# A fused attention and expert kernel: in the last batch slot, slot reads before first-layer weights, one gather behind two scatters, table operations one step later

## The reference

```python
def reference(x, ctx, mask, g_xattn, g_ffn, adj, Wq, bq, Wk, bk, Wv, bv, Wo, bo, gate_w, w1, b1, w2, b2):
    # attention: 16 heads of 16, scores + adj, masked, softmax over 512 keys
    x = x + tanh(g_xattn[0]) * attention(layernorm(x), ctx, ctx, adj, mask, Wq, bq, Wk, bk, Wv, bv, Wo, bo)
    # experts: each token goes to the one expert with the highest gate probability
    h = layernorm(x)
    probs = softmax(h @ gate_w.T)                  # [2048, 8]
    e, p = argmax(probs), max(probs)
    y = (relu(h @ w1[e] + b1[e]) @ w2[e] + b2[e]) * p
    return x + tanh(g_ffn[0]) * y
```

## Time and profile before

| | |
|---|---|
| median of 3 runs | 548.91 us (548.83 to 552.67) |
| profiled execution, its own time | 550.53 us |
| its span in the profile | 548.5 us |
| granted clock of PE over the span | 0.998 |
| PE busy | 526.3 us, 96% |
| VectorE, ACT, POOL busy | 302.3, 309.1, 297.9 us |
| the last slot's attention ends | about 369.6 us |
| late tiles | from 414 us to the end |

### The profile page before, as it was taken

One profiled execution on the slowest core, in us unless ns is written; L12 is line 12 of the kernel. 1 busy time (PEld: TensorE's weight loads), 2 busy tenths in 40 slices (PEclk: granted clock), 3 DMA queues, 4 the chain that ended last, 5 costly groups with the idle time before them and its releaser, 6 DMA issues. The chain is left out here.

```text
span 548.5 us, 13306 instructions
## 1 busy us (share of the span) xinstructions
PE 526.3 (96%) x4123; PEld 405.1 (74%) x4124; DVE 302.3 (55%) x923; ACT 309.1 (56%) x678; POOL 297.9 (54%) x424
## 2 busy tenths in 40 slices
PE   8999999989999999999999999888999999999997
PEld 5577667667666667666676666658899999999996
DVE  2776587976677887668885878845340211111111
ACT  4366678665678665778675676664332333333322
POOL 5346566665567575468574556555244444443451
PEclk9999999999999999999999999999999999999999
DMA  8633625400405510204520057499136665555570
GB/s 288 206 110 132 192 65 183 149 31 6 150 21 192 166 50 1 79 10 153 180 85 1 11 184 250 147 362 320 59 103 218 211 205 196 178 187 184 189 210 1
DMA packets 51489, 77.67 MB, mean 142 GB/s; under 512 B 9945, under 2 KB 34601, under 8 KB 51305
## 3 DMA queue, kind: packets, MB, share of 16 engines
q1 hardware_dynamic: 46600, 67.72, 37.0%
q0 software_dynamic: 4192, 8.73, 5.0%
q10 hardware_dynamic: 640, 0.52, 0.3%
HBM read 52.76 MB, written 8.35 MB: 111 GB/s over the span
## 5 line engine op out<-in xcount | busy, mean ns | idle before, releaser
L1588 DVE CUSTOM_DVE_ANT_0 prob<-bank,adjm 128x512 f32<-128x512 f32 x256 | 172.3, 688 | 70.6 <-issue 39.9
L1229 ACT ACTIVATE pt<-bank 128x512 f32<-128x512 f32 x256 | 152.1, 596 | 87.7 <-PE bank L951 81.2
L682 POOL TENSOR_SCALAR prob<-prob,negmax 128x512 f32<-128x512 f32 x190 | 132.0, 698 | 117.6 <-DVE negmax L1588 113.4
L951 PE MATMUL bank<-ident,prob 128*128 128x128 f32 x1024 | 154.8, 274 | 2.2 <-POOL prob L682 1.3
L951 PEld LDWEIGHTS bank<-ident,prob 128*128 128x128 f32 x1024 | 124.2, 141 | 39.7 <-issue 13.7
L1299 ACT ACTIVATE adjm<-bank,colsm 128x128 f32<-128x128 f32 x184 | 52.6, 368 | 105.0 <-PE bank L1127 80.0
L940 PE MATMUL bank<-w2s 128*128 128x512 bf16 x256 | 97.5, 381 | 8.5 <-DVE negmax L1588 5.7
L963 PE MATMUL bank<-pt,vals 128*32 128x256 f32 x1024 | 68.3, 385 | 0.9 <-DVE vals L1386 0.5
L1127 PEld LDWEIGHTS bank<-xT,pt 128*128 128x128 f32 x576 | 67.1, 192 | 0.9
L1127 PE MATMUL bank<-xT,pt 128*128 128x128 f32 x576 | 67.2, 275 | 0.0
L1137 PE MATMUL bank<-w2s,adjm 128*128 x288 | 65.1, 379 | 0.0
(11 more groups left out here) (195 smaller groups left out, 624.4 us busy)
## 6 DMA issues: line engine op xcount, KB each, us to landing
pt<-in_L_ffn_w SPq DMA_DIRECT2D x19, 1024.0 KB
w2s<-parts SPq DMA_DIRECT2D x96, 128.0 KB
w2s<-in_L_ffn_w SPq DMA_DIRECT2D x8, 1024.0 KB
maski<-in_mask_Bx1xSxS_ik SPq DMA_DIRECT2D x4, 1024.0 KB, 5.6
w2s<-parts SPq DMA_DIRECT2D x56, 64.0 KB, 2.1
xres<-in_x SPq DMA_DIRECT2D x18, 128.0 KB
x_d<-rows SPq DMA_DIRECT2D x18, 128.0 KB
xn_d<-rows SPq DMA_DIRECT2D x18, 128.0 KB
```

Source lines behind the costliest of these rows:

```text
L682: po.tensor_scalar(prob[:, m], prob[:, m], -1.0, negmax[:, m:m + 1], ALU.mult, ALU.add).then_inc(s_shpool, 1)
L951: mm = pe.transpose(tr_bank[n % NTB][:, c * P:(c + 1) * P], prob[:, n % TILES % NB, c * P:(c + 1) * P], ident[:])
L1229: act.activation(pt[:, g % 2, :, j, q2 * P:(q2 + 1) * P], tr_bank[c % NTB][:].rearrange("p (c q) -> p c q", c=QT), ACT.Exp).then_inc(s_cac ...
L1588: ve.tensor_tensor_reduce(out=prob[:, m % NB], in0=sc_bank[m % NS][:], in1=adjm[:, qt], scale=-1.0, scalar=BIG, op0=ALU.add, op1=ALU.min, ...
```

## The change

Three places change, and nothing that is computed:

- TABLE_STEPS: the first five of the twelve table steps of the last slot stand one step later on VectorE (42 to 46 instead of 41 to 45). The other seven stay.
- INDEX_STEP: the copy of the token numbers is at step 58 instead of 59 (TILES - 6); the first gather of normalized rows stays at 59. On SP the wait for the scatters and the five slot reads come ahead of the three weight loads.
- After the slot, POOL issues the two gathers of normalized rows of tiles 3 and 4 one after the other, then early_x(1); early_x(2) moves behind the two scatters and the two tail_rstd pairs.

```diff
@@ -130,8 +130,8 @@
-    TABLE_STEPS = (41, 42, 43, 44, 45, 48, 49, 50, 51, 52, 65, 66)
-    INDEX_STEP, NORMED_STEPS = TILES - 5, (TILES - 5, TILES - 2)
+    TABLE_STEPS = (42, 43, 44, 45, 46, 48, 49, 50, 51, 52, 65, 66)
+    INDEX_STEP, NORMED_STEPS = TILES - 6, (TILES - 5, TILES - 2)
@@ -489,12 +489,12 @@
             sp.wait_ge(e_eid, 1)
             sp.wait_ge(s_xT, B * 4)
-            for s in range(3):
-                early_w1(s)
             sp.wait_ge(r_scat, B * (16 * QT))
             for s in range(EARLY):
                 at = sp.value_load(base_i[0:1, s:s + 1], min_val=0, max_val=X * TOK)
                 sp.dma_start(slots[:, s], slot_d[ds(at, P), 0:2]).then_inc(e_slots, 16)
+            for s in range(3):
+                early_w1(s)
             sp.wait_ge(s_score, last * TILES + 6 * TILES // 8)
@@ -732,15 +732,14 @@
             wait_apart(po, s_osb, B * GROUPS + 2)
             early_normed(3)
+            early_normed(4)
             early_x(1)
-            early_normed(4)
-            early_x(2)
             pairs(B, B)
             for t in range(*RANKED[0]):
                 to_slots(t)
             for k in range(2):
                 tail_rstd(B, k)
-            for s in range(3, EARLY):
+            for s in range(2, EARLY):
                 early_x(s)
```

## The result

| | before | after |
|---|---|---|
| median | 549.83 us (548.83 to 552.67, 8 runs) | 554.33 us (552.66 to 555.99, 8 runs) |
| ratio, 95% interval | | 1.0089 [1.0068, 1.0109] |
| profiled execution, span | 550.53, 548.5 us | 553.77, 552.0 us |
| mean granted clock of PE, profiled execution | 0.998 | 0.996 |

The forecast was 548.9 (547.3 to 550.6). It started from the median of three runs of the kernel before, 548.91; over eight runs that kernel has 549.83. So of the 5.4 us between forecast and result 0.9 are the starting point and 4.5 the change.

What follows compares the result with a forecast made beforehand. TensorE, busy 96% of the span, was taken as the bound. The terms -0.05 + 0 + 0 + 0 took the profiled 550.53 to 550.48; the median 548.91 less 0.05 gave 548.9, range 547.3 to 550.6.

Steps and rivals of the forecast that it cites:

- part two: Weight loads on SP's queue go out 5.6 us later but still land before PE wants them: 0.
- Slack 1.1 to 1.9 us: 0: Second-layer blocks land at 380.8 to 381.6, PE first wants them at 382.68, so lateness costs 0.
- So that block landed at about 375.2 before: Last second-layer block's landing in the kernel before, from 8.65 MB at 352 GB/s; 376 with six gathers.
- second-layer weights late: Rival: PE waits at its first second-layer matmul, 382.73; priced 1.4 at 310 GB/s, 549.7 us taken; chance 0.18.
- the hold: PE's unexplained 1.67 us at two tiny transposes, 375.01; as a rival, dropped 547.2 or doubled 550.5; chance 0.14.
- Part four: Five table pairs on VectorE one step later; its sum unchanged, cost 0, bounds a gain or loss of 0.6 us.
- the third rival: PE's unexplained stall at 375 moves: dropped gives 547.2, doubled 550.5; chance 0.14, half each way.
- Part one: Slot reads ahead of weights, index copy one step earlier: PE's 0.85 us gap closes, gain 0.05 us.
- the gap of 0.85 us: PE's idle before step 61's transposes at 364.42; forecast to close, with only 0.05 us of it gained.
- Exp 60 hangs on transposes that the change does not move: ACT's exp of step 60, 363.86, stays put, so the last exp ends only 0.05 us earlier.
- Part three: POOL's gathers reordered around the two scatters behind the slot; no scatter moves, no reader waits: 0.
- The first rival: The 0.85 us PE gap before step 61's transposes comes back whole: 548.1 us; chance 0.16.

Runs made afterwards that it cites:

- e6: Kernel after with tile 2's first-layer weight load moved behind the last second-layer load and the old table steps; 550.14 us, ratio 1.0012.
- e1: Kernel before with only the new SP order and the index copy one step earlier; 553.17 us, ratio 1.0013.
- e12: The kernel of e1 once more, in another group of runs beside the kernel before; 555.06 us, ratio 1.0097.
- e10: Kernel after with the table steps put back as before; 554.02 us, ratio 1.0082.
- e11: As e10, with 18 spare matmuls on PE ahead of its wait for the second-layer weights; 552.04 us, ratio 1.0041.
- e14: Kernel before with only the changed order of POOL's gathers behind the slot, a repeat in another group; 549.98 us, ratio 1.0003.
- e7: Kernel before with both gathers of x rows (tiles 1 and 2) behind the two scatters; 549.71 us, ratio 0.9996.
- e4: Kernel after with tile 2's first-layer weight load moved behind the last second-layer load; 551.95 us, ratio 0.9995.
- e2: Kernel before with only the table steps moved (42 to 46); 553.33 us, ratio 1.0018.

## Why the prediction was wrong

**The step that failed** is the end of part two: "Slack 1.1 to 1.9 us: 0", and in it first of all the sentence "So that block landed at about 375.2 before". The rival *second-layer weights late* came true, at its place and by its mechanism, but at 1.96 us of wait (priced at most 1.4), with a fall of the clock (unpriced), and with a chance of 0.18. PE wanted the block at 382.07 and could start at 384.03; forecast were a landing at 381.6 (six gathers) and a wish at 382.68. The slack was -1.96 instead of 1.1, and the 3.0 us between are 1.2 of a landing that was read too early, 1.2 of a later start, and 0.6 of an earlier wish (the hold's 1.62 less the 0.84 by which the weighing came later than forecast, and 0.17 of small rows):

- *In the kernel before the block landed at 377.2, not at 375.2 or 376.* The forecast counted megabytes. The packets say it directly: second-layer blocks move in packets of 1 KB, first-layer weights in packets of 4 KB. The DMA view of the kernel before for 376.4 to 376.7 and 376.7 to 378.0 us:

```profile
DMA packets 35, 0.12 MB, mean 413 GB/s; under 512 B 1, under 2 KB 6, under 8 KB 35
DMA packets 138, 0.50 MB, mean 384 GB/s; under 512 B 16, under 2 KB 16, under 8 KB 138
```

  The kernel after, for 383.0 to 383.3 and 383.3 to 384.3 us:

```profile
DMA packets 39, 0.13 MB, mean 421 GB/s; under 512 B 3, under 2 KB 10, under 8 KB 39
DMA packets 138, 0.42 MB, mean 418 GB/s; under 512 B 37, under 2 KB 37, under 8 KB 138
```

  The last packets of 1 KB (5 and 7 of them) stand in the first row of each pair, and there are none in the second. The last completion that each trace has for these loads is at 377.18 and at 383.84. With 377.2 the forecast's own sum is 377.2 + 5.6 = 382.8, behind the wish of 382.68: the slack was gone by this term alone. And the change did not make the stream longer: from SP's first weight load to the last completion it is 28.05 us before (from 349.13) and 27.84 after (from 356.00). The stretches of the two kernels, before and after:

```profile
350.60:377.20 26.60, 21.83 (x205) 15.72 (x203) 15.29 (x56) 14.68 (x33) 14.04 (x21) 1.00 1.03 354
357.40:384.00 26.60, 22.45 (x204) 17.67 (x204) 13.55 (x53) 14.39 (x38) 14.54 (x21) 1.00 1.05 371
```

  In 26.6 us they moved 26.6 x 0.354 = 9.42 MB and 26.6 x 0.371 = 9.87 MB, not 8.65 or 8.9. I had counted only what is issued ahead of the last second-layer block. The DMA view of the kernel after for 381 to 384 us shows the rest:

```profile
DMA packets 603, 1.18 MB, mean 394 GB/s; under 512 B 79, under 2 KB 396, under 8 KB 603
```

  603 - 396 = 207 packets of 4 KB, 0.85 MB, nearly all of the weights of tiles 3 and 4, issued at 377.53 and 378.69 (the gathers' queue moved 0.01 MB in this time), went through while the last second-layer block was still not complete. So what is issued ahead of a block, divided by the rate, gives too early a landing. Whether the later loads also delay the block is not shown; a megabyte less ahead of it does bring it forward, to 25.2 us behind the first weight load in e6. My rival used the rule of the Trainium skill ("DMA: Bandwidth & Descriptors", Queues, rings and completion order), that descriptors on one engine are taken in ring order, to say that the blocks can't pass the three weight loads. The same page of the Trainium skill (Two DMAs through the same engine are not ordered) says that nothing orders transfers across the 16 engines. So some engines can be at later loads while another still has a part of the block; the packets agree with both, and I had read only the first.
- *The start was 1.21 later than before for another reason than the reads*: 0.45 is the table steps. Part four was put at 0 with bounds of 0.6, and the value lies inside them, but not for the reason given there (a lead of 0.6 carried and given back): the rows above show two operations held beside POOL's shifts. The other 0.76 was there ahead of all that the change touches and delays PE's wish as well.
- *The wanted time held a hold of its own.* 382.73 in the trace of before came after the unexplained 1.67 us at 375. Without it PE wants the weights at 381.1 (382.73 less the 1.62), and even the forecast's landing at 380.8 to 381.6 has a slack of about 0. I listed the hold as a rival by itself, "it may drop: 547.2", and never asked what its going would uncover. e1 and e12 are this sum in the same code: held 2.01, wait 1.56; held 0.28, wait 2.85. So the third rival's sign was wrong too: the dropped hold gained nothing, since PE waited for weights in its place.

**What no term held** is the granted clock: behind the wait it cost 1.78 us in the profile of after. Of the 2.3 to 2.9 us that spare matmuls give back it is the part that the traces show; the rest stays open.

**Part one** was right in its mechanism, with a size off: the copy's wait and the gap of 0.85 us are gone, and ACT, not POOL, is next. The gain is 0.42 instead of 0.05. In ACT's timeline of the kernel after:

```profile
363.72 0.71 ACT L1254 ACTIVATE prob<-prob,negmax 128x512 f32<-128x512 f32 x1
364.81 0.60 ACT L1228 ACTIVATE pt<-bank 128x512 f32<-128x512 f32 x1 [0.38 <-PE bank L950]
365.31 0.71 ACT L1254 ACTIVATE prob<-prob,negmax 128x512 f32<-128x512 f32 x1
365.92 0.59 ACT L1228 ACTIVATE pt<-bank 128x512 f32<-128x512 f32 x1
```

Exp 60 starts at 364.81; by the later base_i it would be 363.86 + 1.21 = 365.07. "Exp 60 hangs on transposes that the change does not move" was wrong by 0.25 us: the profile of after shows the transposes of steps 60 and 61 in one row of eight on PE. e6, e10 and e11 have 32.78 or 32.79 us from positions to weighing, against 33.20 before and 33.12 in e14, where this part is as before. The reads landed in 1.6 to 1.7 us (1.8 taken), the copy came in time; these were right.

**Part three** was right: e14 1.0003, e7 0.9996, and the scatters still behind an idle POOL.

**The first rival** (the gap comes back whole) fell: 0.42 of 0.85.

## What to carry to other kernels

A slack is the difference of two times, and each has to be freed of what the profile can't explain: a wanted time that lies behind an unexplained stall of the consumer is an upper bound, and the sum has to be made once without that stall. When small reads go ahead of a saturated stream, find the last block of the stream that someone waits for and read its landing from its packets or completions in the trace, not from a count of megabytes: here it moved by 6.7 us when the stream's start moved by 6.9, and the count had been 1.2 us short. Then move the block that is wanted last to the end (e4, e6) instead of giving up the early reads. Here a wait of PE of 1.96 us was followed by a fall of the clock that cost 1.78: price both, and look at the mean clock of several runs.

## What the runs showed of the hardware that was not expected

- The clock of PE after a pause is not the same in each execution: it fell to 0.54 and 0.61 behind 1.96 us of idle (after) and to 0.50 behind 2.01 (e2), and stayed at 1.00 behind 2.85 (e12), 2.24 (e10) and 1.56 (e1). The mean clock of the single runs shows that a profile of one of them can mislead: e12's is the quickest of seven.
- PE is held 1.7 to 2.0 us ahead of two tiny transposes in some executions (1.90 in the kernel before, 2.01 in e1) and 0.28 in others (e12, the kernel of e1). PE's release is VectorE's operation L1503. That stands behind L1500, which in the kernel before started at 376.67 after 2.78 us of idle, and which waits for matmuls of PE that had started by 375.01, 1.7 us earlier. Why their end is seen so late was not found.
- Two or six numbers per row on VectorE took 0.52, 0.62 or 1.20 us instead of 0.17 beside POOL's shifts.
- Slot reads landed in 1.6 to 1.7 us with no weights in flight, against 4.2 to 7.5 beside them.
- Packets of loads that were issued 6.6 and 7.7 us later on the same queue (377.53 and 378.69, against 370.95) moved while the earlier load was not complete: 0.85 MB of them in its last 3 us.
